# ScalarE instead of VectorE unpacks the sixteen mask units of the first pass of a graph-attention kernel

## The reference, cut to what matters

```python
xt = jnp.einsum('ni,hio->hno', x, W)
src = jnp.einsum('hnf,hf->hn', xt, a[:, :out_f])
dst = jnp.einsum('hnf,hf->hn', xt, a[:, out_f:])
e = jax.nn.leaky_relu(src[:, :, None] + dst[:, None, :], 0.2)
e = jnp.where((adj_matrix > 0)[None], e, -jnp.inf)
attention = jax.nn.softmax(e, axis=2)
h_prime = jnp.einsum('hij,hjf->hif', attention, xt)
out = layernorm(x + h_prime.transpose(1, 0, 2).reshape(n, 256))
```

## Time and profile before

| what | value |
|---|---|
| time, median of 3 executions | 2212.24 us (2212.24 to 2214.11) |
| time of the profiled execution | 2213.66 us |
| its span, first to last instruction | 2212.1 us |
| PE busy | 2108.5 us (95%) |
| DVE busy | 2069.6 us (94%) |
| ACT busy | 2011.0 us (91%) |
| POOL busy | 89.6 us (4%) |
| mean granted TensorE clock | 0.988 |
| shares of the chain that ended last | PE 51%, DVE 21%, ACT 10%, issue 9% |

### The profile page before, as it was taken

How to read it: one execution, slowest core, us unless ns; L and a number is a source line. 1 busy time by engine, 2 the same in 40 slices (tenths; PEclk the granted TensorE clock), 3 DMA queues, 4 the chain that set the end, 5 groups by cost and what they waited for, 6 DMA issues and landing times.

```text
span 2212.1 us, 79064 instructions
## 1 busy us (share of the span) xinstructions
PE 2108.5 (95%) x34304; PEld 2056.8 (93%) x34304; DVE 2069.6 (94%) x2288; ACT 2011.0 (91%) x2053; POOL 89.6 (4%) x88
## 2 busy tenths in 40 slices
PE   8768999999999999999999999999999999999996
PEld 4658999999999999999999999999999999999996
DVE  3899999999999999999999999999999999997775
ACT  3466998999999999999999999999999999999995
POOL 0110000010000100010000100010000100000000
PEclk9989999999999999999999999999999999999998
DMA  9699777766766676666766676666766677532310
GB/s 315 223 349 380 266 246 246 238 213 212 250 213 217 208 248 206 216 212 214 249 212 212 208 231 224 216 211 212 250 212 216 203 233 239 164 83 84 96 46 20
DMA packets 236441, 469.64 MB, mean 212 GB/s; under 512 B 14704, under 2 KB 22896, under 8 KB 236080
## 3 DMA queue, kind: packets, MB, share of 16 engines
q1 hardware_dynamic: 231600, 447.53, 61.8%
q0 software_dynamic: 4352, 16.78, 2.1%
q10 hardware_dynamic: 128, 0.13, 0.0%
HBM read 438.83 MB, written 25.56 MB: 210 GB/s over the span
## 4 chain that ended last, share of the span: by engine, by line
PE 51%; DVE 21%; ACT 10%; issue 9%; DMA 1%; DVEq 1%; POOL 0%; ACTq 0%; SPq 0%; POOLq 0%
PE acc L835 48%; ACT big L433 9%; DVE big L623 7%; DVE big L630 6%; PE tp L801 3%; DVE nat L539 2%; DVE big L615 1%; DVE stats L676 1%; ACT big L477 1%; DVE AT L553 1%; DVE big L637 1%; DVE nat L537 1%; DMA raw<-in_adj_dram 0%; DMA v_parts<-big 0%; DVE big L645 0%
## 5 line engine op out<-in xcount | busy, mean ns | idle before, releaser
L433 ACT ACTIVATE big<-big,d_all 128x1024 int8<-128x1024 f32 x1792 | 1896.5, 1141 | 84.0 <-PE acc L835 84.0
L835 PE MATMUL acc<-big 128*128 128x130 f16 x32768 | 1911.8, 220 | 30.4 <-DVE big L637 28.8
L835 PEld LDWEIGHTS acc<-big 128*128 128x128 fp8e5 x32768 | 1888.2, 98 | 39.7 <-issue 37.2
L623 DVE SCALAR_TENSOR_TENSOR big<-big,AT 128x1024 uint32<-128x1024 uint32 x512 | 627.2, 1225 | 62.1 <-ACT big L433 60.6
L630 DVE SCALAR_TENSOR_TENSOR big<-AT,big 128x1024 uint32<-128x1024 uint32 x512 | 626.7, 1224 | 4.3
L801 PE MATMUL tp<-ident,nat 128*128 128x128 f32 x1024 | 158.5, 278 | 41.9 <-DVE nat L537 33.0
L615 DVE TENSOR_SCALAR big<-big,d_all 128x1024 uint8<-128x1024 f32 x256 | 193.2, 755 | 0.0
L537 DVE TENSOR_SCALAR nat<-raw 128x2048 fp8e4<-128x2048 int32 x128 | 176.3, 1380 | 3.8 <-DMA raw<-in_adj_dram 3.8
L539 DVE TENSOR_SCALAR nat<-raw 128x2048 uint8<-128x2048 int32 x128 | 178.1, 1391 | 0.0
L553 DVE SCALAR_TENSOR_TENSOR AT<-AT,tp 128x512 uint32<-128x512 uint32 x224 | 154.8, 691 | 1.5
L801 PEld LDWEIGHTS tp<-ident,nat 128*128 128x128 f32 x1024 | 108.9, 142 | 49.2 <-DVE nat L537 38.8
(11 more groups left out here) (50 smaller groups left out, 377.9 us busy)
## 6 DMA issues: line engine op xcount, KB each, us to landing
raw<-in_adj_dram SPq DMA_DIRECT2D x256, 1024.0 KB, 5.7
big<-v_parts SPq DMA_DIRECT2D x512, 260.0 KB, 3.7
v_parts<-big SPq DMA_DIRECT2D x16, 1040.0 KB, 5.2
big<-s_rows SPq DMA_DIRECT2D x32, 512.0 KB, 5.5
AT<-in_x_dram SPq DMA_DIRECT2D x16, 512.0 KB, 6.5
big<-in_x_dram POOLq DMA_DIRECT2D x8, 1024.0 KB, 7.5
out_dram<-big POOLq DMA_DIRECT2D x8, 1024.0 KB, 9.0
big<-in_L_gnn_W_dram SPq DMA_DIRECT2D x2, 128.0 KB, 2.5
```

The source lines that it names most:

```text
L433: return nc.scalar.activation(sgn[:, g % NB, b, :], srow[:, h % 2, :], ACT.Sign, bias=dflat[:, r:r + 1], scale=-1.0)
L623: nc.vector.scalar_tensor_tensor(out=word(sgn, g % NB), in0=word(sgn, g % NB), scalar=EDGE[plane], in1=edges(g), op0=ALU.bitwise_and, op1= ...
L835: return nc.tensor.matmul(acc[:, k, o:o + 2 * VO], m[:, g % NB, b, t * P:(t + 1) * P], Vr[:, v:v + 2 * VO], start=opens, stop=False, skip_ ...
```

## The change

ACT unpacks units 16 to 31 with `keep_first`, and DVE does not any more. On ACT the unpacking of the units made in stage g - 4 stands ahead of the signs of stage g, for g from 4 to 15; that of unit 31, made in stage 12, comes behind the signs of stage 15. `kept_at` gives DVE only units of the next chunk, from stage 18 on, and `keep` loses its branch for a fresh `AT` (L551). That branch also cleared the bits that are not edges, with an AND; ACT's copy keeps the whole word, and L623 and L630 take their bit by an AND as before.

```diff
         def kept_at(first, after_first, s):
             if first:
-                return [k for z in range(max(0, s - 2), s - 1) for k in made_at(True, z)]
+                return [k for k in made_at(True, s - 2) if k >= 0] if s >= NG + 2 else []
...
                     for g in range(len(SIGNS_WITH) if first and h == 0 else 0, NG):
+                        if first and h == 0:
+                            for k in made_at(True, g - 4):
+                                keep_first(UN + k)
                         act.wait_ge(sums_done, p * NG + g + 1)
...
+                    if first and h == 0:
+                        for z in range(NG - 4, NG):
+                            for k in made_at(True, z):
+                                keep_first(UN + k)
...
-            def keep(k, u, plane, fresh=False, n=0, g=0):
+            def keep(k, u, plane, n, g):
...
-                if fresh:
-                    nc.vector.tensor_scalar(to, of, EDGE[0], None, ALU.bitwise_and).then_inc(at_done, 1)
-                else:
-                    nc.vector.scalar_tensor_tensor(out=to, in0=to, scalar=EDGE[1 - plane], in1=of,
-                                                   op0=ALU.bitwise_and, op1=ALU.bitwise_or).then_inc(at_done, 1)
+                nc.vector.scalar_tensor_tensor(out=to, in0=to, scalar=EDGE[1 - plane], in1=of,
+                                               op0=ALU.bitwise_and, op1=ALU.bitwise_or).then_inc(at_done, 1)
```

More of the change, by code:

```diff
@@ L539, in convert @@
                     nc.vector.tensor_scalar(to, of, 0.0, 59.0, ALU.is_gt, ALU.add).then_inc(conv_done, 1)
-            def keep(k, u, plane, fresh=False, n=0, g=0):
+            def keep(k, u, plane, n, g):
                 dve.wait_ge(tp_done, k + 3)
-                if not fresh:
-                    z = (g - u // 2) % NG
-                    dve.wait_ge(pos_done if z == 0 else neg_done, n + 1 if z == 0 else n - z + 5)
+                z = (g - u // 2) % NG
+                dve.wait_ge(pos_done if z == 0 else neg_done, n + 1 if z == 0 else n - z + 5)
                 to = AT[:, u // 2, :, u % 2, :]
                 of = tp[:, u % 2, :].bitcast(u32).rearrange("p (b i) -> p b i", b=B)
-                if fresh:
-                    nc.vector.tensor_scalar(to, of, EDGE[0], None, ALU.bitwise_and).then_inc(at_done, 1)
-                else:
-                    nc.vector.scalar_tensor_tensor(out=to, in0=to, scalar=EDGE[1 - plane], in1=of,
-                                                   op0=ALU.bitwise_and, op1=ALU.bitwise_or).then_inc(at_done, 1)
+                nc.vector.scalar_tensor_tensor(out=to, in0=to, scalar=EDGE[1 - plane], in1=of,
+                                               op0=ALU.bitwise_and, op1=ALU.bitwise_or).then_inc(at_done, 1)
             for g in range(NG):
@@ L703, in chunk @@
                             if k < 0:
-                                keep(UN * (c + 1) + k, k + UN, plane, first, n, g)
+                                keep(UN * (c + 1) + k, k + UN, plane, n, g)
                                 last[(k + UN) // 2] = UN * (c + 1) + k + 3
                             elif more:
-                                keep(UN * (c + 1) + k, k, 1 - plane, False, n, g)
+                                keep(UN * (c + 1) + k, k, 1 - plane, n, g)
                                 last[k // 2] = UN * (c + 1) + k + 3
```

## The result

The changed kernel takes 2207.84 us (median of 13 executions, 2206.51 to 2209.35), the kernel before 2213.40 us beside it (13 executions): ratio 0.9975, 95% interval 0.9967 to 0.9983, so 5.6 us less (the interval allows 3.8 to 7.3). On a second occasion it was 2207.93 against 2213.43 us, again 0.9975 (0.9966 to 0.9985). In the profiled execution the span is 2206.3 us against 2212.1.

A forecast was written before the change was run, and what follows sets the result against it. In the first pass, from unit 20's load at 178.01 us, VectorE, TensorE and ScalarE nearly tie, ScalarE tightest, with the DMA full. 6.3 - 0.7 = 5.6 us off 2212.24 gives 2206.6 us, range 2204.0 to 2210.4.

The forecast's parts named there:

- the sum's two terms, 6.3 and 0.7: First pass: masks of stage 16 start 6.3 us earlier; 0.7 us of that is given back to a clock drop.
- The anchor: VectorE's convert of unit 20 stays at 178.01 us, after its load; time saved before it becomes waiting, near 5 us.
- Stage 4: TensorE turns unit 22 at 184.89 us, not 188.43, and the sums of stage 4 run from 185.36.
- ScalarE's way: ScalarE's queue, tightest from the signs of stage 8 at 189.20, puts the masks of stage 16 at 227.58 us, not 233.89.
- The price that no row showed: One ScalarE unpacking between signs costs 0.49 us from start to start; at a ceiling of 1.02 the gain is 2.6.
- The ties: ScalarE, TensorE and loads nearly tie: unit 27's convert ends 202.21 against ScalarE's unpacking 202.22; sums of stage 12 end 223.0.
- loads keep their landing times: The DMA queue is full, so each load lands as before however early its buffer is freed; unit 27 at 200.7.
- The clock term: TensorE idles 2.9 us after stage 2, the clock drops, stage 3 loses 1.6 us, the gain 0.7; no-drop rival 0.20.

The follow-up runs named there:

- e1: Changed kernel, but ScalarE makes each of the sixteen first-pass copies twice, the second waiting for the first; 2214.10 us, ratio 1.0005 against the kernel before.
- e7: Changed kernel with the loads of units 20 to 22 issued ahead of table loads of the first pass; 2207.92 us, ratio 0.9976 against the kernel before.
- e6: Changed kernel with early loads of units 20 to 23 and second-pass table reloads and row load put off; 2204.28 us, ratio 0.9961 against the kernel before.
- after_again: The changed kernel unaltered, run again beside the reordered one on one chip; 2207.93 us, ratio 0.9975 against the kernel before.
- after_third: The changed kernel unaltered, run once more for a third profile; 2210.15 us, a single execution.
- e3: Kernel before, but ScalarE unpacks unit 20 alone and VectorE the other fifteen; 2212.28 us, ratio 0.9996 against the kernel before.
- e5: Kernel before, VectorE still unpacking, with loads of units 20 to 23 early and second-pass reloads put off; 2210.29 us, ratio 0.9987 against the kernel before.
- e8: Changed kernel with the second pass's table reloads and row load put off, from stage 9 on; 2206.71 us, ratio 0.9972 against the kernel before.
- e2: Changed kernel, but VectorE makes an unused operation of about 0.6 us where each unpacking stood; 2213.24 us, ratio 0.9998 against the kernel before.
- e4: Kernel before, but ScalarE unpacks units 16 to 23 and VectorE units 24 to 31; 2210.99 us, ratio 0.9989 against the kernel before.
- e6_again: Second run of e6, the changed kernel with both moves of loads; 2204.77 us, ratio 0.9961 against the kernel before.

## Why the prediction was right, and where it was not

- **Time.** Forecast 5.6 us less, 2206.6; measured 5.6 less (0.9975), 2207.84. The median of the kernel before, 2212.24 in three executions, was 2213.40 in thirteen; that is the 1.2 us between the two. That the two gains agree to 0.1 us is luck: the interval alone allows 3.8 to 7.3 us, and of the sum's two terms, 6.3 and 0.7, the second did not show in the profiled execution.
- **The anchor** held: convert of unit 20 at 178.01 before and 178.02 after. The wait before it was 3.89 us and not near 5, since VectorE waited 1.68 us for unit 19 already, before the change 0.66.
- **Stage 4** held: turn of unit 22 forecast for 184.89, measured 184.93; sums of stage 4 from 185.36, measured 185.43.
- **ScalarE's way** held: signs of stage 8 at 189.20 (189.26), unpacking of unit 25 at 201.62 (201.67), turn of unit 27 at 202.36 (202.50), signs of stage 12 at 206.67 (206.83), masks of stage 16 at 227.58 (227.71). The price that no row showed, 0.49, was 0.47 to 0.48. e1 shows that this way has next to no slack.
- **The ties** held: the load of unit 27 cost 0.48 us on DVE and 0.14 us on the way to the turn. That loads keep their landing times was right: unit 27 at 200.9 (200.7), unit 31 at 213.7 in both. e7 and e6 show the tie itself: the early loads alone give nothing, with the reloads put off as well the pass is 2.2 us shorter.
- **The clock term failed** in the profiled execution. The step was "it ends stage 2 about 1.3 us earlier than now" and is then idle for 2.9 us. The low clock at the start of the pass lasted longer in that execution, the sums of stage 0 took 5.76 us instead of 4.57, so the turn of unit 18 came no earlier (169.40 against 169.48) and the idle time was 1.75 us, without a drop. From 165.3 to 167.8 us the granted clock was 1.00 of full speed in the kernel before and 0.50 in the one after. PE's timeline before, for the 4.57 and the 169.48:

```profile
163.71 4.57 PE L835 MATMUL acc<-big 128*128 128x130 f16 x64 [0.23 <-DVE big L630]
169.48 0.63 PE L801 MATMUL tp<-ident,nat 128*128 128x128 f32 x4 [1.20 <-DVE AT L551]
```

In the other two profiles of the changed kernel the sums of stage 0 took 4.41 and 4.73 us and the idle time was 3.11 and 3.60 us, as the step had it; the drop came behind the second alone. Over the three profiles of the changed kernel the term was 0, 0 and about 1.7 us, where I had 0.7 in each. So the 6.2 us of the pass were there in full in the first profile.
- **What I did not foresee** is a loss of 1.5 us at 567 us in that execution, as PE's timeline shows:

```profile
561.33 5.55 PE L838 MATMUL acc<-big 128*128 128x130 f16 x94 [0.64 <-DVE big L640]
568.23 0.73 PE L838 MATMUL acc<-big 128*128 128x130 f16 x10 [1.35 <-issue]
```

TensorE stood for 1.35 us in the midst of the sums of a stage for nothing that the profile shows. From the masks of stage 100 to those of stage 150 it is 197.1 us there and 195.5 to 195.6 in all other profiles, those of after_again and after_third among them. So it belongs to that execution; what it was stays open. Its span is 5.8 us shorter all the same, since the stretch from the masks of stage 300 to the end took 847.4 us, 1.5 less than in the profile before; in the thirteen profiles that stretch takes 847.4 to 849.0 us, in kernels with and without the change. That the median gain is 5.6 and not 6.2 is in keeping with a clock term that comes in some executions, but this is not shown: which had it cannot be told without their profiles, and the interval of the gain is wider than the difference.

## What to carry to other kernels

Where three queues are equally full, follow the one that comes out longest through its own order, from a point that the change cannot move to one behind the stretch; shares of busy time say nothing, and the wait that catches the eye (TensorE's 3.55 us) may only pass to the next unit when it is cured (e3). Ask of each saving which of the other queues has slack for it: a change may be worth nothing alone and something beside another (e7 and e6). And work moved to an engine that seems to have a tenth to spare is priced by its steps on that engine's longest run: here 0.6 us more for each copy lost the whole gain.

## What the runs showed of the hardware

- **Low clock behind idle time, but not by its length alone.** Idle times of TensorE of over 1.3 us in the first pass, from stage 1 on, and what the granted clock did: 3.77, 3.60, 3.55, 3.24, 3.06, 2.93, 2.83 and 2.59 us (e5, after_third, before, e8, e2, e1, e3, e4) went with the 1.2 GHz level; 3.11 us (after_again) and 2.90 us (e4, at 206 us) did not, nor did 1.62 to 1.94 us (before, after, e1, e3, e7, e6_again). What else decides stays open.
- **The low clock does not last equally long, and its price differs with that.** The granted clock was 0.50 from 180 to 183 us in e8 and in after_third; from 183.2 to 186.2 it was 1.00 in e8 and 0.50 in after_third. The sums of stage 3 took 4.70 and 6.15 us. From the convert of unit 20 to the masks of stage 16 it is 49.89 us in e8 and 51.35 in after_third, against 49.69 (after) and 49.52 (after_again) without a drop; e8 has other loads as well, so its 0.2 is not the price of the drop alone. Where VectorE set the pace (e2), sums of 4.69 us cost nothing.
- **The full DMA queue kept its landing times here.** With 388 GB/s moved, unit 27 was issued 1.1 us earlier (188.51 instead of 189.61) and landed at 200.9 instead of 200.7. Asking earlier did not help while bytes with less hurry stood ahead; with these put off (e8) unit 27, issued at 189.27, landed at 197.5.
